# A decoder layer on one core: gates moved into the first slots, keys and values one slot later over two pairs of banks, and two unread products ahead of each group of exponents

## The chip, the core and the metric

The kernel runs on one NeuronCore of a Trainium2 chip. The metric is the device time of one execution in microseconds (us). Engines are named as in the profile: PE is TensorE's matmul, PEld its weight load, DVE VectorE, ACT ScalarE, POOL GpSimd, SP SyncE. SP and POOL also issue the transfers.

## What is computed

The input x is 8 batches of 128 tokens by 256 features. The layer has three parts, each with a layer norm before it and a residual after it:

```
x = x + delta_rule_attention(layernorm(x))      # 16 heads, keys and queries of 128, values of 256
x = x + cross_attention(layernorm(x), ctx)      # 16 heads of dimension 8, 256 x 256 per batch
x = x + experts(layernorm(x))                   # shared one and 8 routed ones, top 2
```

In the first part q, k and v are projections, then a causal convolution of four taps and a silu; alpha and beta are sigmoids of two small projections of x (the gates); per head a state is carried over the 128 tokens: decay by alpha, correction of the error by beta, read by q. In the second part, per batch,

```
k = Wk ctx + bk ; v = Wv ctx + bv ; q = Wq x + bq
dot = mask * (q . k) / sqrt(8) - (1 - mask) * 1e6
out = (softmax(dot) * mask) v
```

The reference builds q, k and v of the second part from a context that doesn't depend on x, so keys and values may be computed before the first part ends.

## The kernel before

All five engines run programs written out by hand, with semaphores between them.

**Start.** x is loaded (L362), normed (L898 to L907, `moments`, `normalize`), turned by PE (L1264), copied by ACT as 32-bit `xt` and 16-bit `xth` (L660, L662); DVE takes the rest `xtl` (L919). PE multiplies `xt` with the gates' weights (L1269), ACT and DVE turn that into the logarithms of the gates, PE sums them over time (L1272), DVE leaves `gcum` and `gcol` (L930, L933). POOL splits the first head's weights into a high and a low 16-bit half (`split`, L455 to L461). DVE also prepares `mask5` and `bias5` for the second part (L924 to L940).

**Slots.** The first part is 32 steps: 16 heads by 2 groups of four batches. The `slots` helper calls `slot(k)` on each engine for c = -3 to 33. A slot holds pieces of five steps, each at its own stage: step c+2 is projected (`proj_`, L1294, four tiles n = 0 to 3 of six products each in the two banks `ubank`), biased by ACT (L697) and convolved by DVE (`tap`, L1004, three passes per tile); step c+1 gets its norms, exponents (`ebank`) and grams; steps c and c-1 solve the triangular system by doubling (`b_t1`, `b_ux`, `c_t1`, `c_ux`), read the values (`z`, L1310) and give the output; `outp` (L1474) of step c-2 is added to x. Within a slot each engine's order is the order of the calls. Slot -2 has only projections, slots 30 and later have none, slots 32 and 33 only the ends of the last steps.

**Keys and values.** `kv(n)` (L1503, L1504) forms the keys of batch bb from the context, masked beforehand by POOL (L548, at the end of slot 29); ACT copies them to 16 bits (`k_split`, L768), DVE stacks high and low parts (`kv_stack`, L1078), `v_proj` (L1480) forms the values and DVE adds the bias (`v_add`, L1065). Four batches lie in slot 30 and four in slot 31. All of them use `ubank`: the values of batch bb-1 are computed ahead of the keys of batch bb, after waiting for their stack.

**Heads.** The second part works through 64 units (16 heads by 4) in one order on PE: `top_scores(n)` (L1584) for DVE's maxima (L1138), `energies(n-9)` (L1605) for ACT's exponents (L817), then `values` (L1619); every four units q's products (L1571, `q_proj`) and a turn of the maxima (L1594). Scores and exponents share three pairs of banks in rotation (`pair_of`, `pair_free`): the exponents of a unit take the pair that the maxima of the unit before free. Scores and energies have 32 rows each, in one of four row strips.

After the heads come the router, the experts and the output.

Of the kernel before, what the change touches and what calls it, by code (L numbers as in the profile page):

```python
# [20 lines left out]
P = 128  # L21
# [100 lines left out]
def build(nc, d, out):  # L122
    with ExitStack() as whole:
# [86 lines left out]
        zrow = zz[0:5].rearrange("p r j n -> p (r j n)")  # L210
# [73 lines left out]
        names = ("x_loaded", "consts_loaded", "xattn_loaded", "experts_loaded", "ffn_loaded", "stored")  # L284
        x_loaded, consts_loaded, xattn_loaded, experts_loaded, ffn_loaded, stored = [sem(n) for n in names]
# [37 lines left out]
        ebank = [bank[2], bank[3]]  # L323
        bt, bx, ctk, cx = [quad[:, n, :] for n in range(4)]
# [35 lines left out]
        def _(sp):  # L360
            for b in range(B):
                sp.dma_start(x1[:, b, :], x_in[:, b, :]).then_inc(x_loaded, 16)  # L362
# [63 lines left out]
        def _(pool):  # L426
# [37 lines left out]
            pool.wait_ge(xn_done, B)  # L464
            split(0, 0, None)
            def slot(k):
# [187 lines left out]
        def _(act):  # L654
            s = nc.scalar
            norm_act(act, 0, slice(0, B))

            for b in range(B):
                act.wait_ge(xt_psum, b + 1)
                s.activation(xt[:, :, b * T:(b + 1) * T], bank[b % 2][:, 0:H].rearrange("p (c t) -> p c t", c=CH), ACT.Copy).then_inc(xt_full, 1)  # L660
# [3 lines left out]
            act.wait_ge(gate_step, 1)  # L664
            s.activation(ga[:], gz[:], ACT.Abs).then_inc(gate_act, 1)
            act.wait_ge(gate_act, 1)
            s.activation(ga[:], ga[:], ACT.Exp, scale=-1.0).then_inc(gate_act, 1)
            act.wait_ge(gate_act, 2)
            s.activation(ga[:], ga[:], ACT.Ln, bias=1.0).then_inc(gate_act, 1)

            def slot(k):
                f, a, b0, b, c, d = [k.at(n) for n in (3, 2, 1, 0, -1, -2)]

# [87 lines left out]
                def k_split(n):  # L761

                    if k.i is None and k.c in (STEPS - 2, STEPS - 1):
                        bb = (k.c - STEPS + 2) * 4 + n
                        for m in range(2):
                            act.wait_ge(k_psum, 2 * bb + m + 1)
                            need(act, k_stack, 2 * bb + m - 1)
                            s.activation(kh[:, 1 - m], ubank[1 - m], ACT.Copy).then_inc(k_high, 1)  # L768
# [19 lines left out]
                bias(1)  # L788
                k_split(1)
# [120 lines left out]
        def _(dve):  # L910
# [5 lines left out]
            for b in range(B):  # L916
# [3 lines left out]
            dve.wait_ge(gate_psum, 1)  # L920
            v.tensor_copy(gz[:], bank[2][:, 0:B * 2 * HK]).then_inc(gate_step, 1)
            dve.wait_ge(xattn_loaded, 16 * 8)
            dve.wait_ge(mask_cast, 1)
            v.tensor_copy(mask5[0:4], maskrow[0:4]).then_inc(mask_cast, 1)  # L924
            v.tensor_copy(biash, biasf).then_inc(bias_cast, 1)
            dve.wait_ge(gate_act, 3)
            dve.wait_ge(gate_step, 1)
            v.scalar_tensor_tensor(out=gl[:].rearrange("p b n -> p (b n)"), in0=gz[:], scalar=0.0, in1=ga[:], op0=ALU.min, op1=ALU.subtract).then_inc(gate_step, 1)
            dve.wait_ge(cum_psum, 1)
            v.tensor_copy(gcum[:].rearrange("p h b -> p b h"), bank[3][:, 0:B * HK].rearrange("p (b h) -> p b h", b=B)).then_inc(gates_done, 1)  # L930
            dve.wait_ge(gates_done, 1)
            dve.wait_ge(gate_step, 2)
            v.tensor_tensor(gcol[:].rearrange("p h b -> p b h"), gl[:, :, HK:], gcum[:].rearrange("p h b -> p b h"), ALU.subtract).then_inc(gates_done, 1)  # L933
            dve.wait_ge(mask_cast, 2)
            m5 = mask5[0:4].rearrange("p b n -> p (b n)")
            v.scalar_tensor_tensor(out=m5, in0=m5, scalar=stackcol[0:4, 3:4], in1=maskrow[0:4].rearrange("p b n -> p (b n)"), op0=ALU.mult, op1=ALU.add).then_inc(mask_ready, 1)
            dve.wait_ge(bias_cast, 1)
            v.tensor_copy(bias5[:], biash).then_inc(bias_cast, 1)
            dve.wait_ge(bias_cast, 2)
            v.scalar_tensor_tensor(out=bias5[0:4].rearrange("p k g n -> p (k g n)"), in0=biash[0:4].rearrange("p k g n -> p (k g n)"),  # L940
                                   scalar=stackcol[0:4, 2:3], in1=biasf[0:4].rearrange("p k g n -> p (k g n)"), op0=ALU.mult, op1=ALU.add).then_inc(bias_ready, 1)

            def slot(k):
                f, a, b0, b, c, d = [k.at(n) for n in (3, 2, 1, 0, -1, -2)]

# [116 lines left out]
                def v_add(bb):  # L1062
                    dve.wait_ge(v_psum, bb + 1)
                    for st in range(2):
                        v.scalar_tensor_tensor(out=vv[:, bb, st], in0=bvrow[:], scalar=maskcol[:, bb, st:st + 1], in1=ubank[0][:, st * P:(st + 1) * P],  # L1065
                                               op0=ALU.mult, op1=ALU.add).then_inc(v_ready, 1)

                def kv_stack(n):

                    if not (k.i is None and k.c in (STEPS - 2, STEPS - 1)):  # L1070
                        return
                    bb = (k.c - STEPS + 2) * 4 + n
                    if n > 0:
                        v_add(bb - 1)
                    for m in range(2):
# [3 lines left out]
                                               in1=ubank[hh], op0=ALU.mult, op1=ALU.add).then_inc(k_stack, 1)  # L1079
# [19 lines left out]
                tap(1, 3)  # L1099
                kv_stack(1)  # L1100
# [7 lines left out]
                tap(2, 3)  # L1108
                kv_stack(3)
                lmul(0)  # L1110
                tap(3, 1)
                if k.i is None and k.c in (STEPS - 2, STEPS - 1):
                    v_add((k.c - STEPS + 2) * 4 + 3)
# [3 lines left out]
                level_b(3)  # L1117

# [136 lines left out]
        def _(pe):  # L1255
# [4 lines left out]
            for b in range(B):  # L1260
                pe.wait_ge(xn_done, b + 1)
                need(pe, xt_full, b - 1)
                for c in range(CH):
                    mm = t.transpose(bank[b % 2][:, c * P:(c + 1) * P], xn[:, b, c * P:(c + 1) * P], ident[:])  # L1264
                mm.then_inc(xt_psum, 1)
            for b in range(B):
                pe.wait_ge(xt_full, b + 1)
                for c in range(CH):
                    mm = t.matmul(bank[2][:, b * 2 * HK:(b + 1) * 2 * HK], xt[:, c, b * T:(b + 1) * T], wab[:, c, :], start=(c == 0), stop=(c == CH - 1))  # L1269
            mm.then_inc(gate_psum, 1)  # L1270
            pe.wait_ge(gate_step, 2)
            t.matmul(bank[3][:, 0:B * HK], tri[:], gl[:, :, 0:HK], start=True, stop=True).then_inc(cum_psum, 1)  # L1272
# [548 lines left out]
```

## Time and profile before

| | us |
|---|---|
| Runs | 937.96, 933.4, 1081.68 (median 937.96) |
| Profiled execution, its own time | 934.79 |
| Its span, first to last instruction | 932.9 |
| Mean granted TensorE clock | 0.94 |

The stages in the profiled execution, by the timeline: the start runs to 32.9 us, where the first projection begins; the slots with projections to about 623 us; slots 30 to 33 to 702.3 us; the heads to about 859.5 us; experts and output to the end. A granted clock of 1.00 is 2.4 GHz and 0.50 is 1.2 GHz; a stretch with a value between holds both.

### The profile page before, as it was taken

To read this page: it belongs to the slowest core of one execution; us is meant where nothing else is said; L and a number is where in the kernel's file an instruction comes from. 1 tells how busy PE (TensorE), PEld (TensorE's weight loads), DVE (VectorE), ACT (ScalarE), POOL (GpSimd) and SP (SyncE) were. 2 spreads that over 40 slices of the span, in tenths; PEclk is the share of its full clock that TensorE was granted. 3 is DMA by queue.
4 is the path that set the end of the run, shared out by engine and by line. 5 is a ranking of instruction groups with operands and counts; after the bars stand their busy time and mean duration, and the time that the engine had idled before them with its cause. 6 is when DMAs were issued, how large, how long until landed. Compare 5 with 4: busy or idle time off the path is not lost.

```text
span 932.9 us, 21903 instructions
## 1 busy us (share of the span) xinstructions
PE 828.1 (89%) x7371; PEld 531.5 (57%) x7408; DVE 719.7 (77%) x1227; ACT 617.8 (66%) x1022; POOL 540.2 (58%) x689
## 2 busy tenths in 40 slices
PE   3578999999999999999999999998867898889997
PEld 2245776677667766777677767765543333323353
DVE  7768888888888888887888788884556756674746
ACT  3377887788778877887888778873230565567522
POOL 6439769678696796886966968574302232322300
PEclk9989999999999999999999999999985777778999
DMA  6202010010110100101101000000001500000000
GB/s 194 57 1 80 1 35 27 11 35 0 34 34 0 34 19 15 34 0 34 34 0 34 10 23 11 2 2 1 1 1 27 94 15 18 16 14 25 10 23 24
DMA packets 34416, 23.98 MB, mean 26 GB/s; under 512 B 5062, under 2 KB 33414, under 8 KB 34235
## 3 DMA queue, kind: packets, MB, share of 16 engines
q1 hardware_dynamic: 31643, 19.00, 7.2%
q0 software_dynamic: 2720, 4.29, 2.2%
q8 instruction: 32, 0.52, 0.2%
q14 instruction: 21, 0.17, 0.1%
HBM read 22.68 MB, written 1.05 MB: 25 GB/s over the span
## 4 chain that ended last, share of the span: by engine, by line
PE 66%; DVE 17%; issue 9%; ACT 5%; POOL 2%; DVEq 1%; DMA 0%; SPq 0%; ACTq 0%; POOLq 0%
PE psum L1294 13%; PE psum L1310 11%; PE psum L1474 6%; DVE y L1004 6%; PE psum L1619 3%; PE psum L1571 3%; PE psum L1364 3%; PE psum L1354 3%; DVE mx L1138 3%; DVE ux L984 3%; PE psum L1382 2%; PE psum L1503 2%; PE psum L1389 1%; PE psum L1392 1%; PE psum L1708 1%
## 5 line engine op out<-in xcount | busy, mean ns | idle before, releaser
L1004 DVE SCALAR_TENSOR_TENSOR y<-psum,cwh,y 128x508 f32<-128x508 f32 (+2 forms) x384 | 281.5, 740 | 18.4 <-ACT y L697 12.4
L491 POOL TENSOR_TENSOR ct<-lm,levels 128x256 f16<-128x256 f32 x224 | 152.0, 701 | 18.4 <-DVE lm L1027 18.4
L477 POOL TENSOR_TENSOR sql<-sq,sqh 128x1024 f16<-128x1024 f32 x32 | 68.4, 2137 | 126.3 <-ACT sq L744 126.3
L697 ACT ACTIVATE y<-psum,cwh 128x512 f32<-128x512 f32 x128 | 99.4, 777 | 50.8 <-PE psum L1294 50.8
L1310 PE MATMUL psum<-wo,vt 128*128 128x256 f32 x512 | 126.0, 389 | 1.2 <-DVE y L1004 1.0
L1310 PEld LDWEIGHTS psum<-wo,vt 128*128 128x128 f32 x512 | 92.3, 190 | 11.9 <-DVE y L1004 2.0
L817 ACT ACTIVATE et<-psum 128x1024 f32<-128x1024 f32 x64 | 65.2, 1022 | 43.3 <-PE psum L1605 43.3
L1138 DVE TENSOR_REDUCE mx<-psum 128x4 f32<-128x1024 f32 x64 | 77.2, 1219 | 21.4 <-PE psum L1584 21.3
L1294 PE MATMUL psum<-xth,whi 128*128 128x512 f16 x256 | 78.0, 387 | 8.7 <-DVE y L1004 5.4
L984 DVE TENSOR_TENSOR ux<-ux,psum 128x512 f16<-128x512 f16 x64 | 43.9, 686 | 53.8 <-PE psum L1392 52.7
L1294 PE MATMUL psum<-xth,wlo 128*128 128x512 f16 x256 | 78.0, 387 | 0.0
L1294 PE MATMUL psum<-xtl,whi 128*128 128x512 f16 x256 | 77.9, 387 | 0.0
L509 POOL TENSOR_TENSOR lml<-lm,lmh 128x1024 f16<-128x1024 f32 x32 | 68.3, 2135 | 0.0
L972 DVE TENSOR_TENSOR ux<-ux,psum 128x512 f16<-128x512 f16 x96 | 65.1, 678 | 1.1 <-PE psum L1392 0.8
L1389 PEld LDWEIGHTS psum<-t1z,ux 128*128 128x128 f16 x768 | 46.9, 98 | 32.4 <-ACT t1z L679 2.5
L1382 PE MATMUL psum<-ux,ct 128*128 128x64 f16 x768 | 54.7, 194 | 11.3 <-DVE ux L984 7.3
L1474 PE MATMUL psum<-zz,pt 128*128 128x256 f32 x256 | 62.4, 388 | 0.7 <-ACT pt L717 0.7
L499 POOL TENSOR_TENSOR lmh<-lm,zero 128x1024 f16<-128x1024 f32 x32 | 60.5, 1891 | 0.0
L1389 PE MATMUL psum<-t1z,ux 128*128 128x64 f16 x768 | 54.3, 194 | 3.4 <-ACT t1z L684 1.9
L595 POOL TENSOR_SCALAR mxs<-mx 128x16 f32<-128x16 f32 x16 | 4.0, 253 | 88.2 <-DVE mx L1138 88.2
L1474 PEld LDWEIGHTS psum<-zz,pt 128*128 128x128 f32 x256 | 49.5, 194 | 7.9 <-ACT pt L717 1.0
L1382 PEld LDWEIGHTS psum<-ux,ct 128*128 128x128 f16 x768 | 36.7, 97 | 30.0 <-DVE ux L984 12.7
(215 smaller groups left out, 2016.6 us busy)
## 6 DMA issues: line engine op xcount, KB each, us to landing
wraw<-in_L_attn_Wv SPq DMA_DIRECT2D x32, 128.0 KB, 2.7
wo<-in_L_attn_Wo SPq DMA_DIRECT2D x16, 256.0 KB, 2.8
wraw<-in_L_attn_Wk SPq DMA_DIRECT2D x16, 128.0 KB, 2.5
wraw<-in_L_attn_Wq SPq DMA_DIRECT2D x16, 128.0 KB, 2.7
moved<-avs SPq DMA_DIRECT2D x128, 16.0 KB, 1.8
x<-in_x SPq DMA_DIRECT2D x8, 128.0 KB, 4.1
maskrow<-in_mask_row POOLq DMA_DIRECT2D x1, 1024.0 KB, 4.5
xt<-in_ctx SPq DMA_DIRECT2D x1, 1024.0 KB, 6.1
```

Source lines behind the costliest of these rows:

```text
L477: g.tensor_tensor(lo, f, hi, ALU.subtract).then_inc(sq_split, 1)
L491: g.tensor_tensor(dst, src, pick.unsqueeze(1).to_broadcast([P, NB, T // (2 * m), m]), ALU.mult).then_inc(masked[l], 1)
L509: g.tensor_tensor(lo, f, hi, ALU.subtract).then_inc(lm_low, 1)
L697: s.activation(y[:, n], ubank[n % 2].rearrange("p (j t) -> p j t", j=NB), ACT.Identity, scale=cwh[:, (a.c // 2) % 2, n, TAPS - 1:TAPS], bi ...
L984: v.tensor_tensor(changed(r, m), changed(r, m), cx.rearrange("p (a q u) -> p a q u", a=2, u=m), ALU.subtract).then_inc(uxc_sb, 1)
L1004: v.scalar_tensor_tensor(out=y[:, n, :, sh:], in0=u[:, :, 0:T - sh], scalar=cwh[:, (a.c // 2) % 2, n, TAPS - 1 - sh:TAPS - sh], in1=y[:, n ...
L1138: v.tensor_reduce(mx[:, h % 2, g2, 2 * rp:2 * rp + 2].rearrange("p r a -> p (r a)"), pair_of("max", n).rearrange("p r (a s) -> p (r a) s", ...
L1294: mm = t.matmul(ubank[n % 2], w_[:, hr, n, ch, :], x_[:, ch, cols], start=(m == 0), stop=(m == len(ops) - 1))
L1310: mm = t.matmul(ubank[n][:, j * H:(j + 1) * H], vt[:, r, vc, (2 * n + j) * T:(2 * n + j + 1) * T], wo[:, hr, vc, :], start=(vc == 0), stop ...
L1382: mm = t.matmul(half(dst[:, j * 64:(j + 1) * 64], m), ct[:, st.c % 2, level, j], first_half(turned(st.c % 2, 1, j), m), start=True, stop=True)
L1389: mm = t.matmul(half(dst[:, 256 + j * 64:256 + (j + 1) * 64], m), turned(st.c % 2, 0, j), first_half(t1z[:, level - 1, j * T:(j + 1) * T], ...
L1474: mm = t.matmul((ctk, cx)[hf][:, jj * H:(jj + 1) * H], pt[:, j], zz[:, d.c % 2, j], start=True, stop=True)
```

## The change

Four edits, all in the order of work; the arithmetic of what is read stays the same.

1. The start: each batch's norm waits for its own load; the ACT table set with both logarithm and exponential is loaded ahead; the turned x goes to `quad`'s banks; POOL splits the first head's weights before it issues the eight transfers of the second part and without waiting for xn; PE begins with the projections of slot -2.
2. The gates' products, logarithms and sums are pieces of slot -2; `norms` of slot -1 waits for them. `bias5` is prepared at the end of slot -1 on DVE, `mask5` at the end of slot 0.
3. Keys and values lie in slots 31 and 32, alternate between `ubank` and `ebank` from batch to batch, and the values of batch bb-1 come after the keys of batch bb.
4. Ahead of each `energies`, behind its wait for the pair, PE multiplies the 16-bit identity with 256 columns of the stacked keys, twice, into the pair that the energies then overwrite. Nothing reads these 128 products.

```
+        kbank = (ubank, ebank)
...
-            for dst, src in ((maskrow[:], d["mask_row"].partition_broadcast(P)),
-                             (wks[:], d["xk"]), (wvt[:], d["xv"]), (stackcol[:], d["stackcol"]), (biasf, d["xbias"]),
-                             (bvrow[:], d["bv_row"].partition_broadcast(P)), (maskcol[:], d["mask_col"]), (wqs[:], d["xq"])):
-                g.dma_start(dst, src).then_inc(xattn_loaded, 16)
...
             pool.wait_ge(conv_scaled, 3)
-            pool.wait_ge(xn_done, B)
             split(0, 0, None)
+            for dst, src in ((maskrow[:], d["mask_row"].partition_broadcast(P)),
...
+            s.preload_act_table_set("natural_log_exp_and_others")
             norm_act(act, 0, slice(0, B))
...
+                def gate_act_():
+                    if k.i is None and k.c == -2:
+                        act.wait_ge(gate_step, 1)
+                        s.activation(ga[:], gz[:], ACT.Abs).then_inc(gate_act, 1)
...
-                    dve.wait_ge(x_loaded, 16 * B)
+                    dve.wait_ge(x_loaded[b], 16)
...
+                def gate_raw():
+                    if k.i is None and k.c == -2:
+                        dve.wait_ge(gate_psum, 1)
+                        v.tensor_copy(gz[:], bank[2][:, 0:B * 2 * HK]).then_inc(gate_step, 1)
+                def gate_sums():
+                    if k.i is None and k.c == -2:
+                        dve.wait_ge(gate_act, 3)
...
+                        dve.wait_ge(cum_psum, 1)
...
+                def prepare_bias():
+                    if k.i is None and k.c == -1:
+                        dve.wait_ge(xattn_loaded, 16 * 8)
...
+                def prepare_mask():
+                    if k.i is None and k.c == 0:
...
                     pe.wait_ge(w_split, a.head + 1)
+                    if k.i is None and k.c in (-2, -1):
+                        pe.wait_ge(xt_low, (k.c + 3) * NB)
...
                     pe.wait_ge(sq_split, b0.count(1, 1))
+                    if k.i is None and k.c == -1:
+                        pe.wait_ge(gates_done, 2)
...
                 def kv(n):
-                    if not (k.i is None and k.c in (STEPS - 2, STEPS - 1)):
+                    if not (k.i is None and k.c in (STEPS - 1, STEPS)):
                         return
...
-                    else:
-                        v_proj(bb - 1)
+                    if bb == 1:
+                        pe.wait_ge(lm_done, STEPS * 2)
                     pe.wait_ge(ctx_masked, bb + 1)
                     for m in range(2):
                         hh = 1 - m
+                        need(pe, k_stack, 2 * (bb - 1))
                         if m == 1:
-                            need(pe, v_ready, 2 * bb)
+                            need(pe, v_ready, 2 * (bb - 1))
                         for g2 in range(2):
-                            o = ubank[hh][:, g2 * H:(g2 + 1) * H]
+                            o = kbank[bb % 2][hh][:, g2 * H:(g2 + 1) * H]
...
                         mm.then_inc(k_psum, 1)
+                    if n > 0:
+                        v_proj(bb - 1)
...
                 proj_(1)
+                gate_products()
...
                 proj_(3)
+                gate_totals()
...
+            def warm(out, b, gq, count):
+                for w in range(count):
+                    t.matmul(out[:, w % 2, 0:H], ident16[:], kst[:, b, gq, :], start=True, stop=True)
...
                 pair_free("exp", n)
+                warm(pair_of("exp", n), b, gq, 2)
```

The new functions on DVE and ACT are the lines that stood ahead of the slots: `gate_raw` is called after `tap(1, 3)`, `gate_sums` after `tap(2, 3)`, `gate_act_` after `bias(1)`, `prepare_bias` and `prepare_mask` at the end of a slot.

How the change moves instructions on PE in the start. The rows are PE's queue from its first product; `ident,xn` turns x, `wab,xt` are the gates' products, `gl,tri` their sums, the others the projections of slot -2. Before:

```order
L1264 MATMUL psum<-ident,xn 128x128 x16
L1269 MATMUL psum<-wab,xt 128x32 x16
L1272 MATMUL psum<-gl,tri 128x128
L1294 MATMUL psum<-xth,whi 128x512 x2
L1294 MATMUL psum<-xtl,whi 128x512 x2
L1294 MATMUL psum<-xth,wlo 128x512 x2
```

Now, the same stretch (two tiles of the projection on either side of the gates' products):

```order
L1290 MATMUL psum<-ident,xn 128x128 x16
L1312 MATMUL psum<-xth,whi 128x512 x2
L1312 MATMUL psum<-xtl,whi 128x512 x2
L1312 MATMUL psum<-xth,wlo 128x512 x2
L1312 MATMUL psum<-xth,whi 128x512 x2
L1312 MATMUL psum<-xtl,whi 128x512 x2
L1312 MATMUL psum<-xth,wlo 128x512 x2
L1321 MATMUL psum<-wab,xt 128x32 x16
```

The gates' sums (`gl,tri`, L1328) now come after all four tiles. On DVE, the end of slot -1 (the last taps of a step, then the second half of `lm`, which POOL and the next slot wait for), as it stands now:

```order
L1025 SCALAR_TENSOR_TENSOR y<-psum,cwh,y 128x4x127
L1025 SCALAR_TENSOR_TENSOR y<-psum,cwh,y 128x4x126
L1025 SCALAR_TENSOR_TENSOR y<-psum,cwh,y 128x4x125
L950 CAST vv<-vv 5x1024
L952 COPY bias<-vv 5x1024
L954 SCALAR_TENSOR_TENSOR bias<-vv,stackcol 4x1024
L1048 TENSOR_TENSOR lm<-psum,decay 128x512
```

Before, `lm` followed the taps at once. On PE in the heads, where scores (`kst,qst`), energies (`qst,kst`) and the turn of the maxima (`ident,mrow`) follow each other, now:

```order
L1627 MATMUL psum<-kst,qst 128x256 x4
L1617 MATMUL psum<-kst,ident 128x256 x2
L1649 MATMUL psum<-qst,kst 128x256 x4
L1637 MATMUL psum<-ident,mrow 128x128 x4
L1627 MATMUL psum<-kst,qst 128x256 x4
```

`kst,ident` are the two unread products; before, the energies followed the scores directly.

## Rows read from the trace of the kernel before

**Rows 1.** The page: TensorE's granted clock in 40 equal slices, in tenths

```profile
PEclk9989999999999999999999999999985777778999
```

**Rows 2.** Busy time by stretch: length, engines, granted clock, DMA share, GB/s

```profile
622.92:657.80 34.88, 30.33 (x225) 20.04 (x222) 17.62 (x35) 13.50 (x27) 17.14 (x22) 0.95 0.00 1
657.80:687.00 29.20, 25.20 (x182) 16.08 (x179) 15.83 (x28) 8.90 (x18) 8.75 (x9) 1.00 0.01 1
687.00:702.30 15.30, 9.48 (x73) 6.74 (x71) 7.26 (x21) 4.13 (x8) 0.00 (x0) 0.62 0.00 0
725.25:831.43 106.18, 93.41 (x872) 33.30 (x872) 70.82 (x81) 61.28 (x76) 28.64 (x81) 0.78 0.18 34
831.43:859.50 28.07, 25.99 (x272) 9.83 (x270) 17.08 (x45) 19.44 (x27) 6.59 (x16) 0.76 0.07 19
```

**Rows 3.** The page's row on a load (us to landing), then the start's timeline (start, length)

```profile
wraw<-in_L_attn_Wv SPq DMA_DIRECT2D x32, 128.0 KB, 2.7
...
9.25 0.98 SPq L376 DMA_DIRECT2D wraw<-in_L_attn_Wv  x2
...
17.43 1.91 POOL L455 TENSOR_TENSOR wraw<-wraw,c 128x1024 f32<-128x1024 f32 x1
17.45 7.48 DVE L919 TENSOR_TENSOR xtl<-xt,xth 128x256 f16<-128x256 f32 x6 [0.22 <-ACT xth L662]
...
19.73 6.88 PE L1269 MATMUL psum<-wab,xt 128*128 128x32 f32 x32
...
22.01 2.31 POOL L461 TENSOR_TENSOR wlo<-wraw,whi 128x1024 f16<-128x1024 f32 x1
...
32.74 2.33 DVE L936 SCALAR_TENSOR_TENSOR mask<-mask,stackcol,maskrow 4x2048 f16<-4x2048 f16 x1
...
32.93 1.01 PE L1294 MATMUL psum<-xth,whi 128*128 128x512 f16 x2 [1.25 <-issue]
...
35.45 3.03 DVE L940 SCALAR_TENSOR_TENSOR bias<-zz,stackcol 4x1024 f16<-4x1024 f16 x1
...
53.56 0.78 ACT L697 ACTIVATE y<-psum,cwh 128x512 f32<-128x512 f32 x1 [2.17 <-PE psum L1294]
...
67.48 0.17 DVE L1048 TENSOR_SCALAR n2m<-psum 128x8 f32<-128x8 f32 x1 [1.87 <-PE psum L1323]
```

**Rows 4.** Slots 30 to 33: two groups by line, then PE's timeline

```profile
L1503 PE MATMUL psum<-xt,wks 128*128 128x256 f32 x64 | 22.2, 429 | 0.7 <-ACT zz L690 0.7
L1480 PE MATMUL psum<-wvt,xt 128*128 128x128 f32 x32 | 6.2, 319 | 3.8 <-DVE kst L1078 3.6
...
633.63 0.28 PE L1382 MATMUL psum<-ux,ct 128*128 128x64 f16 x4 [0.95 <-POOL ct L491]
...
684.73 0.71 PE L1480 MATMUL psum<-wvt,xt 128*128 128x128 f32 x4 [1.25 <-DVE kst L1078]
...
698.48 3.78 PE L1474 MATMUL psum<-zz,pt 128*128 128x256 f32 x8 [0.69 <-ACT pt L717]
```

**Rows 5.** One head period at full clock, one at a mixed clock

```profile
761.30:769.03 7.73, 6.47 (x82) 2.48 (x74) 5.80 (x7) 5.08 (x7) 2.46 (x9) 1.00 0.02 4
...
803.50:813.66 10.16, 8.83 (x74) 3.11 (x74) 5.79 (x6) 5.30 (x8) 1.62 (x5) 0.66 0.10 24
```

**Rows 6.** Chain of waits: products of 512 columns, full clock and half clock

```profile
600.04 1.29 PE psum L1294 x6
...
50.94 5.11 PE psum L1294 x12
```

**Rows 7.** PE's timeline in the heads: scores and energies interleaved, then in sequence

```profile
739.43 0.28 PE L1584 MATMUL psum<-kst,qst 32*128 32x256 f16 x1
...
739.85 0.64 PE L1619 MATMUL psum<-et,vz 128*32 128x256 f32 x8
...
741.05 0.39 PE L1584 MATMUL psum<-kst,qst 32*128 32x256 f16 x4
...
741.66 0.64 PE L1619 MATMUL psum<-et,vz 128*32 128x256 f32 x8
```

More of the change, by code:

```diff
@@ L927, in _ @@
[L927 to L941, printed above, removed]
@@ new lines, in prepare_mask @@
+                def prepare_mask():
+                    if k.i is None and k.c == 0:
+                        dve.wait_ge(xattn_loaded, 16 * 8)
+                        dve.wait_ge(mask_cast, 1)
+                        v.tensor_copy(mask5[0:4], maskrow[0:4]).then_inc(mask_cast, 1)
+                        dve.wait_ge(mask_cast, 2)
+                        m5 = mask5[0:4].rearrange("p b n -> p (b n)")
+                        v.scalar_tensor_tensor(out=m5, in0=m5, scalar=stackcol[0:4, 3:4], in1=maskrow[0:4].rearrange("p b n -> p (b n)"), op0=ALU.mult, op1=ALU.add).then_inc(mask_ready, 1)
@@ L1111, in slot @@
                 tap(3, 1)
[L1112 to L1113 removed]
+                if k.i is None and k.c in (STEPS - 1, STEPS):
+                    v_add((k.c - STEPS + 1) * 4 + 3)
                 tap(3, 2)
@@ L1263, in _ @@
                 for c in range(CH):
-                    mm = t.transpose(bank[b % 2][:, c * P:(c + 1) * P], xn[:, b, c * P:(c + 1) * P], ident[:])
+                    mm = t.transpose(quad[:, b % 2, c * P:(c + 1) * P], xn[:, b, c * P:(c + 1) * P], ident[:])
                 mm.then_inc(xt_psum, 1)
[L1266 to L1272, printed above, removed]
-            pe.wait_ge(xt_low, B)
-            pe.wait_ge(gates_done, 2)
             def slot(k):
@@ L1295, in proj_, with gate_products, gate_totals @@
                     mm.then_inc(proj[n], 1)
+                def gate_products():
+                    if k.i is None and k.c == -2:
+                        for b in range(B):
+                            pe.wait_ge(xt_full, b + 1)
+                            for c in range(CH):
+                                mm = t.matmul(bank[2][:, b * 2 * HK:(b + 1) * 2 * HK], xt[:, c, b * T:(b + 1) * T], wab[:, c, :], start=(c == 0), stop=(c == CH - 1))
+                        mm.then_inc(gate_psum, 1)
+                def gate_totals():
+                    if k.i is None and k.c == -2:
+                        pe.wait_ge(gate_step, 2)
+                        t.matmul(bank[3][:, 0:B * HK], tri[:], gl[:, :, 0:HK], start=True, stop=True).then_inc(cum_psum, 1)
                 def z(n):
@@ L1479, in v_proj @@
                     for st in range(2):
-                        mm = t.matmul(ubank[0][:, st * P:(st + 1) * P], ctxs[:, bb, st * P:(st + 1) * P], wvt[:], start=True, stop=True)
+                        mm = t.matmul(kbank[bb % 2][0][:, st * P:(st + 1) * P], ctxs[:, bb, st * P:(st + 1) * P], wvt[:], start=True, stop=True)
                     mm.then_inc(v_psum, 1)
                 def kv(n):
-                    if not (k.i is None and k.c in (STEPS - 2, STEPS - 1)):
+                    if not (k.i is None and k.c in (STEPS - 1, STEPS)):
                         return
-                    bb = (k.c - STEPS + 2) * 4 + n
+                    bb = (k.c - STEPS + 1) * 4 + n
                     if bb == 0:
@@ L1540, in slot @@
                 b_t1(3)
-                if k.i is None and k.c in (STEPS - 2, STEPS - 1):
-                    v_proj((k.c - STEPS + 2) * 4 + 3)
+                if k.i is None and k.c in (STEPS - 1, STEPS):
+                    v_proj((k.c - STEPS + 1) * 4 + 3)
             slots(pe, slot)
```

70 lines of the change are left out of this document (40 added, 30 removed).

## The prediction, made before the changed kernel ran

> **What bounds the kernel now.** I read the granted clock over the span first, then the busy time by stretch, then the chain of waits and the timeline of the three places that the diff touches. The clock is full through the slots and lower in the last quarter [rows 1]: the 106.18 us stretch of the heads has a mean of 0.78 [rows 2]. A head is four units. Where the clock is full throughout, a head takes 7.73 us; at 0.66 it takes 10.16 us, while DVE's busy time, 5.80 and 5.79 us, is the same [rows 5]. So in the heads PE sets the pace when its clock is down, and PE and DVE take turns when it is up (6.47 and 5.80 busy of 7.73). In the slots with projections nothing of the change acts, and I count them as unchanged. Slots 30 to 33 have PE busy 30.33 of 34.88, 25.20 of 29.20 and 9.48 of 15.30 us [rows 2]: the last two slots are short steps that wait for each other. In the start PE's first projection comes at 32.93 us, behind the gates [rows 3].
>
> **1. The start.** What the first projection needs is the split of the first head's weights and four batches of `xtl`. The weights are issued until 9.25 + 0.98 = 10.2 us and land 2.7 us later, at 12.9. The split took 22.01 + 2.31 - 17.43 = 6.9 us. Now it starts at about 13 instead of 17.43, ends at 20, and the projections start there: 32.93 - 20.2 = 12.7 us sooner [rows 3]. `xtl` could be late: six of them took 7.48 us beside the split [rows 3], one between two of POOL's instructions, so four end by about 18 to 20.5. The gates' products, 6.88 us [rows 3], now stand between the second and the third tile; of these about 3 us fall where PE waited for taps before. ACT's third bias waits for the gates' three activations and the last taps wait for the sums, so the slot gives back about 3 us: the first bias of slot -1, at 53.56 before [rows 3], comes near 43.5, 10 us sooner. Bounds: 7, if the gates' products run at the low clock and delay both following tiles; 12.7, if everything inserted hides.
>
> `bias5` and `mask5` leave the start but go where DVE is dense. Their large instructions took 3.03 and 2.33 us [rows 3]; the three smaller ones I put at 2.3 together from these, 7.6 us in all, 4.1 of it for `bias5`. In slot -1 they stand ahead of `lm`, for which POOL waits and behind which DVE had 1.87 us idle [rows 3]: 4.1 - 1.87 is 2.3 us late. In slot 0 I take as much idle, 3.5 - 1.9 = 1.6, and 0.6 for waiting. Together 4.5 lost; bounds 2 and 7.6. Why 3.03 us for 1,024 columns when 2,048 took 2.33? It ends 1.1 us after an instruction of POOL, as the `xtl` did. Here the Trainium skill (SBUF — State Buffer, section on the two separate sides) says that DVE and GpSimd share a pair of ports as an exclusive lock held for a whole instruction. The trace agrees; by that rule each of the five moved instructions can wait for one of POOL's, which is the upper bound and not my sum. Net of the start: -10 + 4.5 = **-5.5**.
>
> **2. Keys and values.** PE's work is the same: 22.2 us of keys' products, 6.2 us of values' [rows 4], and the bias products. Only its cover changes. Slot 30 loses four batches. The first was free: PE would have waited anyway for POOL's mask, until 633.63 [rows 4]. Behind it the other three took some 14 us of PE and its waits, of which 2 to 3 come back as waits between short steps, and the now longer idle of PE (5 us before 633.63) may lower the clock: slot 30 becomes 11.2 us shorter (9 to 13.5). Slot 31 keeps four; with values behind the next keys and a second pair of banks the waits of `v_proj` for the stack go, except the last of 1.25 us: of 3.8 us in both slots [rows 4] slot 31 had 2.5, and 1.3 go. Slot 32 gains four batches: four by 3.36 + 0.55 = 15.6 us, 1.3 us of wait for the last stack; hidden in the 5.8 us that PE idles in 15.30 [rows 2] are about 5. The last `outp` took 3.78 us at the low clock [rows 4] and, behind dense work, takes 1.8. Sum: 15.6 + 1.3 - 5 - 2 = 9.9 longer. The next reader, POOL's mask of x, waits for all values, so this is on the path. Net: -11.2 - 1.3 + 9.9 = **-2.6** (bounds -7 and +2). The first products of q start at full clock for a moment: **-1**.
>
> **3. The unread products.** A product of 512 columns takes 0.215 us at full clock and 0.426 at half (1.29 / 6, 5.11 / 12 [rows 6]); 256 columns are 0.107 and 0.213. Two per unit cost 0.21 or 0.43 us, 64 units 13.7 or 27.3. They come behind the wait for the pair, so PE's idle time before the energies doesn't hold them. They also stand between scores and energies: interleaved, both take 739.85 - 739.43 = 0.42 us, one after the other 741.66 - 741.05 = 0.61 [rows 7]. Twice per head they interleave. The Trainium skill (TensorE: Matmul & The Clock Gate, section on packing small matmuls) says that a weight load overlaps running matmuls only if their row groups differ; a full-height product between the two strips ends that. By this rule a head pays 8 x 0.107 + 2 x 0.19 = 1.24 us at full clock, by a DVE-bound reading nothing.
> I take 0.5: PE has 7.73 - 6.47 = 1.26 us slack per head, but half of the insertions lie on the way from one maximum to the next scores. What they may buy is the clock. It falls inside the heads although PE is never idle for long, in the stretches with narrow products (32 rows) and no products of q; it holds or rises where full-array products lie close. The unread ones are full-array and lie in every unit. If it holds, each of the 12 heads from 725.25 to 831.43 takes 7.73 + 0.5 = 8.2 us [rows 5] instead of 106.18 / 12 = 8.85 [rows 2]: -7.5. The last stretch, 28.07 us at 0.76 [rows 2], holds 9 energies (+1.9) and would get back 2 to 3. The first two heads have no energies and stay at half clock. Together **-8** (bounds -14, cost hidden, and +5, cost in full).
>
> **The sum**: -5.5 - 2.6 - 1 - 8 = -17. Against the profiled execution's own 934.79 that is **918 us**; it lies 0.3% below the median of 937.96, one of whose three runs was disturbed, so the ratio is best taken to about 935: -1.8%.
>
> **Rivals.** (a) *The products only cost.* The clock in the heads falls as often as before. Then a unit pays 0.31 at full clock and 0.73 at half (0.43 and the lost overlap); with 44% of the stretch at half clock, 64 x (0.56 x 0.31 + 0.44 x 0.73) = 31.7, and 934.8 - 9 + 31.7 = 957 us, slower. It decides if the full-array products of a unit don't suffice; against it: the clock held for up to 20 us on the present work. Chance 0.08. (b) *The clock holds, the products cost in full*: 12 x (7.73 + 1.24) = 107.6, no gain in the heads, 927 us. Chance 0.22. (c) *The moved work costs what it frees*: the start nets -2 (gates' chain through four engines in slot -2, two preparations in dense slots) and keys and values +2, heads as forecast: 926 us. Chance 0.18. (d) *More than forecast*: tables hidden, products hidden in DVE's time, 905 to 913 us. Chance 0.17. Forecast 0.35.
>
> **Numbers.** The range 906 to 932 leaves out (a), the far end of (d) and (b) with (c) together. About 2% is what a measurement can tell here, 18.7 us; the forecast itself sits just inside. Faster by over 2% takes (d) and two thirds of the forecast's own case, since 918 lies on the border whether the ratio is taken to 935 or to the median: 0.4. Slower by over 2%: 0.07. Within: 0.53.
>
> **What would show it.** The first projection near 20 us and the first bias of slot -1 near 43.5; `lm` of slot -1 some 4 us behind its last taps. Slot 30 about 23.7 us, slots 32 and 33 about 25. The granted clock 0.95 or more from about 730 us on and a head at 8.2 us; if it shows 0.8, (a) is right, if it shows 1.00 and a head of 8.9, (b). The prediction would be wrong altogether if the slots with projections, 560 us unchanged by the diff, ran differently.

## The result: 997 us, slower by 6.6%

| | before | after |
|---|---|---|
| Median of the runs shown together | 936.22 us | 996.96 us |
| Profiled execution: own time, span | 934.79, 932.9 us | 997.5, 995.7 us |
| Mean granted TensorE clock | 0.94 | 0.871 |

The ratio is 1.0656, 95% interval 1.0611 to 1.0701; it leaves out one run of the kernel before, of 1081.68 us, far above the others. The forecast was 918 us, range 906 to 932. It was wrong in sign and the time lies outside the range.

The page of the changed kernel, busy time and the granted clock in 40 slices:

```profile
PE 908.6 (91%) x7499; PEld 548.0 (55%) x7536; DVE 722.2 (73%) x1227; ACT 617.4 (62%) x1020; POOL 536.8 (54%) x689
...
PEclk9789999999999999999999999876755555557999
...
L1164 DVE TENSOR_REDUCE mx<-psum 128x4 f32<-128x1024 f32 x64 | 77.7, 1221 | 52.5 <-PE psum L1627 50.8
```

Where the row of before reads 85777778 [rows 1], this one reads 55555557: the clock does not go up and down in the heads, it stays down. DVE, the engine that shared the head's time with PE before, now sits idle for 52.5 us ahead of its maxima, nearly all of it waiting for scores (21.4 us in the same row of the kernel before). The busy time by stretch (length, engines, granted clock, DMA share, GB/s) puts a size to it:

```profile
640.49:672.26 31.77, 29.52 (x182) 18.75 (x179) 15.69 (x28) 9.25 (x18) 8.74 (x9) 0.84 0.01 1
...
709.50:910.80 201.30, 197.52 (x1193) 58.59 (x1192) 98.27 (x112) 75.57 (x92) 38.26 (x110) 0.50 0.11 23
...
738.41:887.87 149.46, 149.46 (x904) 42.62 (x904) 67.22 (x75) 58.56 (x72) 25.48 (x72) 0.50 0.10 19
...
752.00:765.59 13.59, 13.59 (x84) 3.88 (x84) 5.98 (x7) 5.29 (x6) 2.13 (x8) 0.50 0.05 15
```

The first row is slot 31. The second is nearly all of the heads: 201 us at half clock. The third is eleven heads in a row, 149.46 / 11 = 13.59 us each, with PE busy in every one of the 149.46 us; the last is one head. Before, a head took 7.73 us at full clock and 10.16 at a mixed one [rows 5]. PE's timeline of a part of that head (start, length, engine, line, operands, count):

```profile
760.14 1.08 PE L1663 MATMUL psum<-et,vz 128*32 128x256 f32 x8
761.15 1.22 PE L1609 MATMUL psum<-xm,wqs 128*128 128x256 f32 x2
762.31 0.39 PE L1610 MATMUL psum<-mask,bias 4*128 4x256 f16 x1
762.31 0.61 PE L1627 MATMUL psum<-kst,qst 32*128 32x256 f16 x4
762.85 0.61 PE L1617 MATMUL psum<-kst,ident 128*128 128x256 f16 x2
763.39 0.61 PE L1649 MATMUL psum<-qst,kst 32*128 32x256 f16 x4
```

From the first scores of a unit to the next step it reads 0.54 for the scores (762.31 to 762.85), 0.54 for the two unread products, 0.54 for the energies. None carries an idle time in brackets: PE waits for nobody, it is slow. Scores and energies, which interleaved in 0.42 us at full clock [rows 7], never do now.

### The profile page after: what moved, and what is told of

Its sections match the earlier page's. It is cut to its first block and busy times, and to the rows that moved or that the text cites. A ratio compares the mean times of both kernels' runs of the same rounds, so it can differ in the third digit from the quotient of the medians.

```text
span 995.7 us, 22169 instructions
## 1 busy us (share of the span) xinstructions
PE 908.6 (91%) x7499; PEld 548.0 (55%) x7536; DVE 722.2 (73%) x1227; ACT 617.4 (62%) x1020; POOL 536.8 (54%) x689
## 5 line engine op out<-in xcount | busy, mean ns | idle before, releaser
L1164 DVE TENSOR_REDUCE mx<-psum 128x4 f32<-128x1024 f32 x64 | 77.7, 1221 | 52.5 <-PE psum L1627 50.8
L1663 PE MATMUL psum<-et,vz 128*32 128x256 f32 x512 | 64.5, 597 | 0.0
```

The source lines that it names most:

```text
L1164: v.tensor_reduce(mx[:, h % 2, g2, 2 * rp:2 * rp + 2].rearrange("p r a -> p (r a)"), pair_of("max", n).rearrange("p r (a s) -> p (r a) s", ...
L1663: mm = t.matmul(avb[ps, gq // 2 * H:(gq // 2 + 1) * H], vz[:, b % 2, st, r, gq], et[:, gn % 4, r, st], start=(gq == 0 and st == 0), stop=( ...
```

## The experiments

Each ratio is to the kernel before on the same chip, with its 95% interval. Unless said otherwise a kernel starts from the changed one.

**1. Without the unread products.**

```
-                warm(pair_of("exp", n), b, gq, 2)
```

> The changed kernel without the unread products (gates later, keys and values a slot later stay). Theory (the unread products hold the clock down): the heads run as before the change, the granted clock rising and falling with a mean near 0.78, a head 8.8 to 9.0 us; the first product of q comes 3.3 us later than before in the changed kernel's trace, so 938 us (934 to 942). Rival (the denser end of keys and values, or the later start of the heads, brings them into the low clock): the heads stay at half clock without the products too, a head near 10.2 us, 957 us or more.

Measured: 927.77 us, ratio 0.9912 (0.9888 to 0.9935), below the expected 934 to 942 and far from the rival. The 3.3 us of the expectation were misread: the first product of q comes at 705.63 in the changed kernel and at 703.94 before, 1.7 us later, and that delay isn't in this trace, which has it at 701.76. The rest of the change is a small gain; the products alone cost 69 us. The clock, the slots and the heads in its trace:

```profile
PEclk9798999999999999999999999998966597967999
...
619.59:640.90 21.31, 14.91 (x161) 11.96 (x158) 10.03 (x19) 9.08 (x19) 17.06 (x22) 0.84 0.01 2
...
640.90:668.10 27.20, 24.95 (x183) 16.25 (x180) 15.66 (x28) 9.25 (x18) 8.74 (x9) 1.00 0.00 1
668.10:701.76 33.66, 27.85 (x137) 15.85 (x136) 16.85 (x40) 8.91 (x16) 0.88 (x2) 0.75 0.00 0
...
733.00:827.69 94.69, 82.90 (x816) 29.63 (x814) 65.19 (x75) 56.92 (x72) 25.41 (x72) 0.82 0.17 34
...
758.43:766.15 7.72, 6.33 (x74) 2.48 (x74) 5.79 (x7) 5.07 (x6) 2.75 (x9) 1.00 0.04 11
```

The same eleven heads take 94.69 us at a mean clock of 0.82, 8.61 each; it rises to full for the first time at 737 us. So 149.46 - 94.69 = 54.8 of the 69 us lie there. Another 8.2 lie in the next two heads, 2.1 in the two ahead and 1.3 behind the heads. The rest, 3.3 us, was there at the first maxima that are copied: slot 31 took 31.77 against 27.20 us, for it has a stretch at half clock (651 to 662 us) that this execution doesn't have. The unread products come later and can't have caused it.

**2. The products alone on the kernel before.**

```
                 pair_free("exp", n)
+                warm(pair_of("exp", n), b, gq, 2)
```

> The kernel before with the two unread products ahead of each group of exponents and nothing else. Theory: the clock stays at half through the heads, a head 13.6 us, 990 to 997 us. Rival (products and the rest act together): the clock rises and falls as before and a unit pays 0.31 us at full and 0.73 at half clock, 960 to 967 us.

Measured: 998.9 us, ratio 1.0674 (1.0644 to 1.0704). Its page and one head:

```profile
PEclk9989999999999999999999999998555555557999
...
752.11:765.69 13.58, 13.58 (x84) 3.88 (x84) 5.97 (x6) 5.29 (x6) 2.13 (x8) 0.50 0.05 14
```

The time is 2 us above what was expected, the head is the expected one. The other edits are not needed for the loss; the rival falls.

**3. Six in place of two.**

```
-                warm(pair_of("exp", n), b, gq, 2)
+                warm(pair_of("exp", n), b, gq, 6)
```

> The changed kernel with six unread products in a unit in place of two. Theory (the clock is low because the full-array products of a unit lie too thin beside the narrow ones): the clock rises to full within the heads, a head 9 to 10 us, 930 to 950 us: more work and less time. Rival (products only cost, the clock is low for another reason): four more by 0.213 us in each of 64 units at half clock, 54 us more, near 1050 us.

Measured: 955.51 us, ratio 1.0178 (1.0138 to 1.0218), 6 us above the upper end of what was expected and 95 below the rival.

```profile
PEclk9798999999999999999999999989675999999999
...
771.05:780.98 9.93, 9.66 (x98) 4.48 (x98) 5.79 (x7) 5.18 (x6) 2.12 (x8) 1.00 0.04 10
```

Three times the unread work saves 41 us: the clock comes up at 742 us and stays up to the end of the heads. A head is bound by PE (9.66 busy of 9.93) but at full clock. So two products do not fail because products cost too much; they fail because the clock stays down with them.

**4. A single burst.**

```
-                warm(pair_of("exp", n), b, gq, 2)
+                warm(pair_of("exp", n), b, gq, 40 if n == 0 else 2)
```

> The changed kernel with 40 unread products ahead of the first group of exponents only, two ahead of each other as before. They take some 8 us at half clock, 6 with the rise. Theory A (the heads hold whichever clock they enter with: at full clock two products suffice to keep it): the clock is full from about 732 us to the end of the heads, a head 8.2 us, near 934 us. Theory B (two products in sequence with the scores do not hold it either): it falls back to half within a head or two and stays there, near 995 us or above.

Measured: 933.39 us, ratio 0.9996 (0.9972 to 1.002), 64 us less than the changed kernel. PE's timeline at the burst, the page's clock, one head, and the eleven heads behind it:

```profile
721.91 5.71 PE L1617 MATMUL psum<-kst,ident 128*128 128x256 f16 x40
727.55 0.39 PE L1649 MATMUL psum<-qst,kst 32*128 32x256 f16 x4
```

```profile
PEclk9789999999999999999999999997976999998999
...
762.16:770.78 8.62, 7.97 (x82) 2.92 (x82) 5.79 (x7) 5.18 (x6) 3.60 (x10) 1.00 0.04 11
736.30:831.49 95.19, 87.68 (x902) 32.22 (x902) 65.09 (x76) 57.97 (x72) 25.41 (x72) 1.00 0.19 37
```

Forty products at 722 us change all that follows: four energies take 0.39 us in place of 0.61 right behind them, and the next eleven heads run at 1.00 with the same two products per unit that ran at 0.50 for 201 us. The same loop has two steady ways to run, 13.59 and 8.62 us per head, and in these two kernels it keeps the one that it enters with. The head is 0.4 us above the expected 8.2.

**5. The burst and nothing else.**

```
+                warm(pair_of("exp", n), b, gq, 40 if n == 0 else 0)
```

> The changed kernel with the 40 products ahead of the first group of exponents and none elsewhere. Both theories: the clock comes up some 5 us sooner and then rises and falls as in the kernel without unread products (mean 0.85 or so), 928 to 934 us. It is the price of the burst without the pairs of products.

Measured: 935.54 us, ratio 1.0000 (0.9973 to 1.0027), just above what was expected.

```profile
737.72:836.19 98.47, 85.88 (x816) 30.57 (x814) 65.18 (x75) 56.96 (x72) 25.38 (x72) 0.80 0.18 35
```

Without the pairs the clock falls and rises again after the burst (0.80), 98.47 / 11 = 8.95 us per head. So once the clock is up, the pairs do hold it, as the prediction had it; what they buy (98.47 - 95.19 = 3.3 us in one profile each) does not show in the totals of runs 4 and 5, whose intervals overlap.

**6. Four.**

```
+                warm(pair_of("exp", n), b, gq, 4)
```

> Four unread products in a unit. By the run with six (a head 9.93 us at full clock, each product 0.107 us, 0.43 us per head): if the clock rises with four too, a head is 9.93 - 0.86 = 9.07 us and the time 955.5 - 14 = 941 us. Rival (four are still too thin): stuck at half clock, 997 + 27 = 1024 us.

Measured: 973.2 us median, its four runs from 941.34 to 981.16, so no ratio is given. The shortest is what the theory expected; none comes near the rival's 1024. One execution (980.9 us) was profiled:

```profile
PEclk9789999999999999999999999898755556998999
...
782.34:797.62 15.28, 15.28 (x92) 5.07 (x92) 5.97 (x6) 5.29 (x6) 2.13 (x8) 0.50 0.05 13
845.90:855.18 9.28, 8.80 (x90) 3.71 (x90) 5.79 (x8) 5.42 (x7) 2.95 (x6) 1.00 0.07 19
```

It has both ways in one execution: half clock until 826 us with heads of 15.28 us (13.59 + 8 x 0.213 = 15.29), then full with 9.28. So the low way isn't kept for good with four, and the spread of 40 us between runs of one program suggests that the moment of the rise varies; only this one trace shows it.

**7. One, still between scores and energies.**

```
+                warm(pair_of("exp", n), b, gq, 1)
```

> The changed kernel with one unread product in a unit in place of two, still between the scores and the exponents. Theory (what keeps the clock low is that scores and exponents no longer overlap, which stretches each unit by 0.54 us at half clock; the product itself gives back less than that): stuck at half clock, a head 13.59 - 4 x 0.213 = 12.74 us, near 985 us. Rival (the harm goes with the number of products): half the harm of two, the clock rises and falls, 940 to 965 us.

Measured: 981.66 us, ratio 1.0506 (1.0449 to 1.0563).

```profile
759.51:772.23 12.72, 12.72 (x80) 3.76 (x80) 5.98 (x6) 5.42 (x7) 2.94 (x6) 0.50 0.04 10
```

12.72 us, as expected from 13.59 less four products. One is nearly as bad as two; the rival, harm by the number of products, falls. Among products between scores and energies one and two leave the clock down, four let it rise late in the profiled execution and six early (runs 3 and 6), so the amount matters as well: a little work there is worse than none and worse than much.

**8. The same two, ahead of the scores.** Scores and energies are neighbours again; all 64 units have the pair, the first nine too, which have no energies beside them.

```
                 pair_free("max", n)
+                warm(pair_of("max", n), b, gq, 2)
...
-                warm(pair_of("exp", n), b, gq, 2)
```

> The changed kernel with the same two unread products of each of the 64 units moved ahead of the scores, into the banks of the maxima, so that scores and energies stand side by side again. Theory (the lost overlap of scores and energies is what stretches the unit and thins the products): at half clock a unit is 0.54 us shorter, its products denser, and the clock rises; a head 8.0 to 8.3 us, 920 to 932 us. Rival (two products only cost wherever they stand): the clock stays at half, a head 13.59 - 4 x 0.54 = 11.4 us, near 960 us.

Measured: 927.61 us, ratio 0.9931 (0.9909 to 0.9953), 69 us below the changed kernel with the same number of products. The page's clock, PE's timeline of one unit, and the busy time of one head:

```profile
PEclk9798999999999999999999999998966599997999
...
766.79 0.39 PE L1617 MATMUL psum<-kst,ident 128*128 128x256 f16 x2
767.12 0.28 PE L1628 MATMUL psum<-kst,qst 32*128 32x256 f16 x2
767.13 0.28 PE L1649 MATMUL psum<-qst,kst 32*128 32x256 f16 x2
...
767.45 0.64 PE L1663 MATMUL psum<-et,vz 128*32 128x256 f32 x8
```

```profile
763.37:771.40 8.03, 7.49 (x82) 2.85 (x82) 5.79 (x8) 5.18 (x6) 3.58 (x10) 1.00 0.04 11
```

The interleaving is back in two of a head's four units, as before the change (a score and an energy start 0.01 us apart), the clock rises at 739 us without any burst and holds for the next 106 us, and a head takes 8.03 us against 8.62 with the pair between, at the same clock. So the lost overlap costs 0.6 us per head at full clock.

Is it the overlap that brings the rise, or the pairs in the first nine units, which no kernel above has? The trace speaks against the pairs: from 707.00 to 738.56 us, through all nine of those units and five more, PE is busy for 30.56 of 31.56 us and the clock is 0.50 throughout. It rises behind units whose scores and energies overlap (at 733 and 737 us), and so it does in run 1 at 737 us with no unread product at all. What the pairs ahead of the scores change is what follows: run 1 falls back to half clock several times, this kernel doesn't. No run takes the overlap away without adding products, so what its loss alone does to the clock stays open; shown is that the same pair is harmless ahead of the scores and costs 69 us between scores and energies.

**9. Another stationary operand.** The identity is nearly all zeros; here a dense piece of the keys takes its place.

```
-                    t.matmul(out[:, w % 2, 0:H], ident16[:], kst[:, b, gq, :], start=True, stop=True)
+                    t.matmul(out[:, w % 2, 0:H], kst[:, b, gq, 0:T], kst[:, b, gq, :], start=True, stop=True)
```

> The changed kernel with a 128x128 piece of the stacked keys as the stationary operand of the two unread products in place of the identity, which is nearly all zeros. Theory (what counts is that the array is used, and the products are too few): stuck at half clock as before, a head 13.59 us, near 997 us. Rival (a product with the identity does not count as work for the clock): the clock rises, a head 8.6 us, near 940 us.

Measured: one execution, 992.86 us, and again

```profile
760.91:774.49 13.58, 13.58 (x84) 3.88 (x84) 5.98 (x6) 5.41 (x7) 2.94 (x6) 0.50 0.03 9
```

The zeros are not the reason, as far as one execution shows it; its head is the same to 0.01 us.

**10. The start alone.** Keys and values in their old slots and banks, no unread products.

```
-        kbank = (ubank, ebank)
+        kbank = (ubank, ubank)
...
-                    if not (k.i is None and k.c in (STEPS - 1, STEPS)):
+                    if not (k.i is None and k.c in (STEPS - 2, STEPS - 1)):
```

> The start of the change alone on the kernel before (gates, masks and biases later; keys and values in their old slots, no unread products). Theory: z of slot 30 comes 3.6 us sooner and nothing behind it changes, 931 to 932 us. Rival (the head start is lost to the clock or at the POOL mask further on): 935 us.

Measured: 933.15 us, ratio 0.996 (0.9928 to 0.9992): by the ratio 3.7 us, interval 0.7 to 6.7, between theory and rival. The read of the values with which the stretch of slot 30 begins is at 619.80 us, 3.1 sooner than before [rows 2]. In this trace the lead doesn't last: slot 31 is at half clock from about 664 to 674 us, which it isn't before, and the first product of q comes at 705.03, 1.1 us later than before. The rival's path exists too.

**11 and 12. Unread products where PE waits anyway.** From the kernel without pairs, 12 products ahead of each of the first two heads' products of q, 6 ahead of each of the first nine units' scores, all into the bank of the values; from the tenth unit on two (run 11) or one (run 12) ahead of the scores.

```
+            def fill(count):
+                for w in range(count):
+                    t.matmul(avb[:, w % 2 * H:(w % 2 + 1) * H], ident16[:], kst[:, 0, 0, :], start=True, stop=True)
             for h in range(2):
+                fill(12)
...
+                if n < LAG:
+                    fill(6)
                 if n < UNITS:
                     top_scores(n)
...
                 pair_free("max", n)
+                if n >= LAG:
+                    warm(pair_of("max", n), b, gq, 1)
```

> Unread products where PE waits anyway: 12 ahead of each of the first two heads' products of q, 6 ahead of each of the first nine units' scores (the first heads ran at half clock until 737 to 742 us in every kernel so far); from then on two ahead of the scores. If the heads keep the clock they enter with, it is full from about 705 us on, a head 8.03 us as with two ahead of the scores, the first three heads 6 to 8 us shorter: 919 to 923 us. Rival (the fill delays the scores or does not lift the clock): 926 to 930 us.

> The same with one unread product per unit ahead of the scores from the tenth unit on. If one holds the full clock, a head is 7.87 us and the time 2 us below the run with two, 917 to 921 us; if it does not, the clock rises and falls with a mean near 0.85 and the head is near 8.4 us, 924 to 929 us.

Measured: with two 926.25 us, ratio 0.9876 (0.9829 to 0.9923), above the expected 919 to 923; with one 921.06 us, ratio 0.9841 (0.9801 to 0.9882), as expected. The page's clock, with two and with one, then a head and eleven heads with one:

```profile
PEclk9798999999999999999999999998769799999999
...
PEclk9789999999999999999999999997989899999999
...
758.21:766.13 7.92, 7.16 (x78) 2.75 (x78) 5.79 (x8) 5.18 (x6) 3.60 (x10) 1.00 0.04 10
734.02:822.29 88.27, 79.79 (x863) 30.45 (x862) 65.19 (x76) 58.18 (x72) 24.98 (x72) 0.99 0.19 38
```

The version with one is the fastest: 1.6% below the kernel before. One product holds 0.99 over eleven heads, 88.27 / 11 = 8.02 us each, where the kernel with no pairs has 0.82 and 8.61.

The fill did hold the clock, and the heads did not keep it: from 692 us on it is full, past the 703 to 709 us at which it falls in runs 1 and 4 and the changed kernel; then it falls at 728.6 us with one product and at 729.6 us with two, within the first heads behind the end of the fill, and comes back at 735 and 740 us. So a loop entered at full clock can still lose it, against the theory of the expectation. In the run with two this stretch at half clock (10.5 us against 6.5) is one cause of the miss; the other lies ahead: slot 31 again had a stretch at half clock (652 to 662 us) and the first product of q came at 706.68, 2.5 us later than with one.

## Why the prediction was wrong

**The step that failed** stands in part 3: "If it holds, each of the 12 heads from 725.25 to 831.43 takes 7.73 + 0.5 = 8.2 us". The condition was taken as likely because "the unread ones are full-array and lie in every unit". That counts what is added and not what it does to the rest. What happened in its place: the heads stayed at 0.50 for 201 us and took 13.59 us each. The same part priced the lost overlap of scores and energies as time, 0.19 us, for the two units of a head that had it. That is too little: in the same place of a head the two groups take 0.42 us interleaved (before) and, leaving out the products between them, 0.42 + 0.32 = 0.74 apart (765.77 to 766.19 and 766.52 to 766.84 in run 4) at full clock, and 0.74 (run 1) and 0.75 + 0.54 = 1.29 (changed kernel) at half. The 0.61 that the prediction took for the sequence was of a unit whose energies start 0.29 us behind the scores, so part of the overlap was in it. And it is more than time: heads at half clock got out of it before, and with one or two products between scores and energies they do not (runs 1, 2, 7, 8). That this is because PE then spends more of each unit on narrow products, one strip at a time, fits these runs; it is a reading, and no run separates it. The prediction asked whether the clock holds and never whether it rises at all, although it said itself that "the first two heads have no energies and stay at half clock": the heads with pairs begin in the low state. (In the changed kernel the clock falls to half at 709 us, 16 us ahead of the first unread product.)

**Part 3's other steps.** That two per unit hold the full clock was right (run 4). The cost at full clock was 8.62 - 7.72 = 0.90 us per head, between the 0.5 taken and the 1.24 of the full price; so even where the clock holds, the term of -8 was 933.39 - 927.77 = +6 by the times and +8 by the ratios 0.9996 and 0.9912 (with the burst's 5.71 us in it). The Trainium skill's rule, as cited in the prediction (TensorE: Matmul & The Clock Gate, section on packing small matmuls), is that a weight load overlaps running products only where the row groups differ. The trace agrees as far as it goes: no score and energy start within 0.05 us of each other in the changed kernel's heads, while in the kernel before and in run 8 they do in two units of a head.

**Rival (a)**, the products only cost, had the sign and a chance of 0.08. Its 957 us are 40 short, since it left the clock's share as it was (44% at half) and let it fall "as often as before". Its own price at half clock, 4 x 0.73 = 2.9 us on top of the head of 10.16 us [rows 5], gives 13.1, and that head was not yet all at half; measured are 13.59. **Rival (b)**, 927 us, is nearest to the kernel with a burst (run 4, 933.39 us; 0.90 per head against its 1.24). **(c)**, that the moved work costs what it frees, has something in it for the start (below); **(d)** describes no run.

**Part 1, the start: the gain was right, the price of the preparations half of what it was.** The first projection came at 20.26 us (forecast 20); the split ended already at 18.8, and what came last was `xtl`. The first bias of slot -1 came at 41.09 (43.5). `bias5` took 52.54 to 56.68 us, 4.1 as forecast:

```profile
20.26 1.01 PE L1312 MATMUL psum<-xth,whi 128*128 128x512 f16 x2 [2.56 <-DVE xtl L924]
...
23.38 0.59 PE L1312 MATMUL psum<-xtl,whi 128*128 128x512 f16 x2
...
24.25 3.65 PE L1321 MATMUL psum<-wab,xt 128*128 128x32 f32 x32
...
41.09 0.78 ACT L701 ACTIVATE y<-psum,cwh 128x512 f32<-128x512 f32 x1 [0.91 <-PE psum L1312]
...
52.54 2.39 DVE L950 CAST vv<-vv 5x1024 f16<-5x1024 f32 x1
54.96 0.41 DVE L952 COPY bias<-vv 5x1024 f16<-5x1024 f16 x1
55.41 1.27 DVE L954 SCALAR_TENSOR_TENSOR bias<-vv,stackcol 4x1024 f16<-4x1024 f16 x1
...
74.34 2.60 DVE L962 CAST mask<-maskrow 4x2048 f16<-4x2048 f32 x1
76.97 2.34 DVE L965 SCALAR_TENSOR_TENSOR mask<-mask,stackcol,maskrow 4x2048 f16<-4x2048 f16 x1
79.24 0.67 DVE L1048 TENSOR_TENSOR lm<-psum,decay 128x512 f32<-128x512 f32 x1
80.64 0.17 DVE L1069 TENSOR_SCALAR n2m<-psum 128x8 f32<-128x8 f32 x1
```

The gates' products took 3.65 us, not 6.88 [rows 3]. The granted clock reads 1.00 in both stretches, but the durations don't: a weight load of theirs took 190 ns here and 333 before, and two products of 512 columns went from 1.01 us at 20.26 to 0.59 at 23.38. By these durations PE was at half clock for the gates before and at full clock now, behind the projections.

That `bias5` took 4.1 us as forecast is luck in the parts. Its first cast took 2.39 us and 0.67 before: POOL's instruction beside it ran from 52.26 to 54.39 us, where POOL had been idle before. Its last took 1.27 us and 3.03 before [rows 3], now with POOL idle. The cast of `mask5` took 2.60 us beside an instruction of POOL and 1.20 before. So in these rows an instruction of DVE is 1.4 to 1.8 us longer when one of POOL's runs beside it, a wait that the prediction named and left out of its sum.

`n2m` is a small instruction of the norms, soon behind `lm` in each slot. Its start shows where the 12.5 us that the first bias had gained went. In slot -1 it is 9.45 us sooner than before (58.03 against 67.48): 3.0 lost, 2.3 forecast. In slot 0 it is 4.90 us sooner (80.64 against 85.54): 4.55 more lost, nearly all of the 4.94 us of `mask5`, where 2.2 were forecast. In slot 1 it is 3.4 us sooner (100.84 against 104.26), and so it stays to slot 30 (619.35 against 622.92, 3.6). So the preparations and what followed gave back 8.9 us, twice the 4.5 of the forecast and beyond its bound of 7.6; the idle time of DVE that I had counted on in slot 0 wasn't there. Forecast -5.5; measured by the ratio of run 10 -3.7 (interval -6.7 to -0.7).

**Part 2, keys and values: wrong in sum by the trace.** Against [rows 2], slot 30 lost 13.6 us (11.2 forecast), slot 31 2.0 (1.3), by the trace of run 1. Slots 32 and 33 to the first product of q took 33.66 us against 703.94 - 687.00 = 16.94: +16.7 where +9.9 stood. That is -13.6 - 2.0 + 16.7 = +1.1 in these two executions where -2.6 stood. The term that was mis-sized is the price of the four batches in slot 32: at a granted clock of 0.75 the keys of the first two took 5.2 and 5.8 us (671.45 to 676.6 and 679.14 to 684.9), not the 3.36 of the forecast, which is 4.3 of the 6.8 us. The first products of q and what follows took 15.7 us to the first complete q against 16.7: -1.0, as forecast.

**The three together** were forecast at -9.1, and run 1 measured 935.83 - 927.77 = -8.1 (interval -6.1 to -10.5). That is luck in good part. In the two profiles, which differ by 6.8 us, the first turn of the maxima comes at 716.51 against 719.71 us, 3.2 sooner; another 2.1 us lie between the first and the last turn and 1.5 behind them, where the forecast put nothing and where the clock rises and falls in both kernels. Keys and values by themselves are the difference of runs 1 and 10, some -4.5 us by the ratios with intervals that overlap, against +1.1 by the traces; their size stays open.

## What to carry to other kernels

A loop can have two steady ways to run, a fast and a slow one, with the same instructions. Ask of an edit not only whether it holds the high clock but whether the low one can still be left with it, and in which one the loop is entered. In this kernel a little unread work was harmless ahead of a group or where PE waited anyway, and did its harm between two groups of products that overlap each other. And a PE that is 100% busy in the profile is no proof that it is fast: read the clock beside it, and at the start of a program the durations too.

## What the runs showed of the hardware

- PE stayed at 1.2 GHz for 201 us, 149 of them without a single gap in the profile; 40 full-height products in 5.71 us brought the same loop to 2.4 GHz for the next 95 us. The Trainium skill (TensorE: Matmul & The Clock Gate, section on the clock gate) has a busy engine warm up and only an idle one fall back. The trace disagrees here: PE was busy 149.46 of 149.46 us at a clock of 0.50.
- More work of the same kind in the same place was faster: two, four and six products per unit gave 997, 973 (941 to 981) and 956 us. None at all gave 928.
- A clock that is full at the entry of the heads can be lost: in runs 11 and 12 it fell some 37 us after it had risen, for 10.5 and 6.5 us.
- At the start of the program the column of the granted clock reads 1.00 where the durations are those of half clock: 1.01 us for two products of 512 columns at 20.26 us, 0.59 at 23.38.
- The changed kernel and those of runs 1, 11 and 12 have the same instructions up to the heads, and yet some of their executions have a stretch at half clock of some 10 us in slot 31 (652 to 662 us in the profiles of the changed kernel and of run 11) that others don't have; it moves everything behind by 3 to 5 us. A difference of single profiles below that says little.
